# A first stage on one core: the order of its first and last tiles, and its results stored by SyncE's queue instead of GpSimd's

## The reference, cut to what matters

```python
def _L0_cond_ref(x, adapter_mapping, W, b, lora_As, lora_Bs):
    base_out = jnp.einsum('bti,oi->bto', x, W) + b
    A = lora_As[adapter_mapping]          # one of 32 adapters for each batch row
    Bm = lora_Bs[adapter_mapping]
    lora_h = jnp.einsum('bti,bir->btr', x, A)
    lora_out = jnp.einsum('btr,bro->bto', lora_h, Bm)
    return base_out + lora_out * SCALING

x = x + _L0_ffn_ref(_L0_cond_ref(x, itok_B_0_23, ...), L0_ffn_W_gate, L0_ffn_W_up, L0_ffn_W_down)
x = x + _L1_ffn_ref(_L1_cond_ref(x, itok_B_0_7, ...), ...)
```

## Time and profile before

| | |
|---|---|
| median of 3 runs | 974.24 us (974.02 to 5092.53) |
| the profiled execution | 974.92 us |
| its span, first to last instruction | 973.2 us |
| TensorE busy | 964.7 us, 99% of the span |
| VectorE, ScalarE, GpSimd busy | 62%, 49%, 29% |
| granted clock of TensorE | 1.00 of full speed |
| DMA, mean over the span | 229 GB/s |

### The profile page before, as it was taken

The page is one execution under the profiler, slowest core; times in us unless marked ns, Lnnn a source line. Parts: engine busy times, 40 slices in busy tenths (PEclk is TensorE's granted clock), DMA queues, the critical chain, the costliest instruction groups (busy, mean ns, idle before and its releaser), DMA issues.

```text
span 973.2 us, 14085 instructions
## 1 busy us (share of the span) xinstructions
PE 964.7 (99%) x4659; PEld 814.8 (84%) x4659; DVE 605.5 (62%) x1027; ACT 472.1 (49%) x877; POOL 285.8 (29%) x380
## 2 busy tenths in 40 slices
PE   9999999999999999999999999999999999999998
PEld 7888888888888888888888888888888999898986
DVE  5785987877973333785332497333378487785862
ACT  4765766664832333671333383333357274535342
POOL 5984225544202611500713220351150460000000
PEclk9999999999999999999999999999999999999999
DMA  7787476776879876877877768986688650616132
GB/s 238 269 334 263 129 259 237 294 284 237 312 264 321 281 195 194 280 259 254 292 247 196 241 225 266 323 281 193 192 291 289 244 190 23 238 46 215 65 108 87
DMA packets 112081, 222.78 MB, mean 229 GB/s; under 512 B 12165, under 2 KB 12166, under 8 KB 111370
## 3 DMA queue, kind: packets, MB, share of 16 engines
q1 hardware_dynamic: 108576, 211.37, 65.0%
q0 software_dynamic: 3296, 10.51, 3.0%
q10 hardware_dynamic: 138, 0.01, 0.0%
HBM read 160.49 MB, written 61.34 MB: 228 GB/s over the span
## 4 chain that ended last, share of the span: by engine, by line
PE 91%; DVE 3%; POOL 2%; DMA 2%; issue 1%; SPq 0%; POOLq 0%; ACT 0%; ACTq 0%; DVEq 0%
PE bank L2132 90%; POOL a_raw L1001 2%; DMA a_table<-in_a_cols 1%; DMA c_scratch<-c_out 1%; PE bank L2302 1%; SPq L653 0%; DVE cop_lo L1693 0%; POOL c_scratch L1047 0%; POOLq L992 0%; POOLq L1000 0%; DVE xa L1594 0%; POOL b_raw L907 0%; DVE wring L1660 0%; DVE hg L1911 0%; DVE h_masked L1634 0%
## 5 line engine op out<-in xcount | busy, mean ns | idle before, releaser
L2132 PE MATMUL bank<-cop_hi,wring 128*128 128x512 f32 x1234 | 380.4, 389 | 0.0
L2132 PEld LDWEIGHTS bank<-cop_hi,wring 128*128 128x128 f32 x1234 | 231.6, 188 | 48.1
L2132 PE MATMUL bank<-cop_lo,wring 128*128 128x512 f32 x616 | 239.6, 389 | 0.0
L2132 PE MATMUL bank<-op_hi,wring 128*128 128x512 f32 x560 | 173.7, 389 | 0.0
L1739 DVE TENSOR_TENSOR v<-bank,p7s 128x512 f32<-128x512 f32 x44 | 30.4, 692 | 197.1 <-PE bank L2132 197.1
L2132 PEld LDWEIGHTS bank<-cop_lo,wring 128*128 128x128 f32 x616 | 115.6, 188 | 24.0
L2132 PEld LDWEIGHTS bank<-op_hi,wring 128*128 128x128 f32 x560 | 105.1, 188 | 21.8
L2132 PE MATMUL bank<-op_lo,wring 128*128 128x512 f32 x280 | 108.9, 389 | 0.0
L1243 ACT ACTIVATE s<-bank 128x512 f32<-128x512 f32 x44 | 26.3, 597 | 114.2 <-PE bank L2132 114.2
L2132 PE MATMUL bank<-xa,w_hi 128*128 128x512 f32 x256 | 76.1, 391 | 1.1 <-ACT c_out L1140 1.1
L947 POOL TENSOR_TENSOR h_t<-h,h 128x512 f32<-128x512 f32 x20 | 27.3, 1365 | 162.2 <-DVE h L1761 162.2
(11 more groups left out here) (253 smaller groups left out, 1844.4 us busy)
## 6 DMA issues: line engine op xcount, KB each, us to landing
wring<-wgu_scratch SPq DMA_DIRECT2D x231, 256.0 KB, 3.0
wring<-wd_scratch SPq DMA_DIRECT2D x140, 256.0 KB, 5.7
wgu_scratch<-wring SPq DMA_DIRECT2D x77, 256.0 KB, 3.4
xs_raw<-x_scratch SPq DMA_DIRECT2D x16, 512.0 KB, 5.8
out<-res SPq DMA_DIRECT2D x32, 256.0 KB, 2.1
wd_scratch<-dt SPq DMA_DIRECT2D x14, 512.0 KB, 4.9
x_raw<-in_x SPq DMA_DIRECT2D x13, 512.0 KB, 5.9
c_scratch<-c_out POOLq DMA_DIRECT2D x24, 256.0 KB
```

The source lines that it names most:

```text
L2132: return e.matmul(out_ap, lhs, rhs, start=start, stop=stop, skip_group_check=True)
```

## The change

It has five edits; TensorE's program is not touched.

1. SyncE, start: block k = 2 of x of tile 1 is loaded behind `a_table` instead of ahead of it.
2. The stores of c go from GpSimd's program to SyncE's. In a tile they alternate with `store_down`; `load_down(1)` comes behind the stores of tile 1; the seven `store_gate_up` and `load_gate_up(2)` come behind the stores of the last tile.
3. GpSimd: the three small loads (b0, b1, languages) are issued ahead of the first gather; `load_slots` and `pick_a` of tile t + 3 follow the gather of tile t + 2.
4. ScalarE and VectorE, tiles 0 and 1: `lora_turn(0, (0,))` and `lora_in(0, (0,))` ahead of `turn_b(0)`; `turn_a(1, (1,))` ahead of the first `close_c`; `turn_b(1)` behind the second `close_c` on ScalarE and behind `turn_a(1, (1,))` on VectorE; `lora_turn(1, (1,))` ahead of the third `close_c`.
5. VectorE, last tile: of the four `gate_up_lo` that stood ahead of `lora_in(7)`, two come between `lora_in` and `lora_rest`, the other two and `gate_up_sums(1)` behind the operands of the second stage.

```diff
--- before.py
+++ after.py
@@ -571,8 +571,7 @@
 
     def ab_hi_n(t, what, g):
 
-        order = "a0", "b0", "b1", "a1"
-        return 2 * NG * t + (order if t == 1 else sorted(order)).index(f"{what}{g}") + 1
+        return 2 * NG * t + ("a0", "a1", "b0", "b1").index(f"{what}{g}") + 1
 
     def a_n(t, g=NG - 1):
         return NG * t + g + 1
@@ -824,9 +823,11 @@
             load_x(0, ks)
             part = slice(ks[0], ks[-1] + 1)
             e.dma_start(w0_raw[:, part, :], w0[:, part, :]).then_inc(w0_in[ks[0]], DMA)
-            load_x(1, ks[:1])
+            if ks[0] < 2:
+                load_x(1, ks)
         e.dma_start(a_table[:, :, :], a_cols).then_inc(a_table_in, DMA)
-        load_x(1, [KC - 1])
+        for ks in x_parts(1)[2:]:
+            load_x(1, ks)
         for t in range(NT):
             if t == 0:
                 for ks in x_parts(2):
@@ -841,15 +842,19 @@
                 e.wait_ge(b_in, NG * DMA * 2)
                 for ks in x_parts(3):
                     load_x(3, ks)
-            if t < 2:
-                load_down(t)
-            if t == NT - 1:
-                for n in range(7):
-                    store_gate_up(n)
-                load_gate_up(2)
-            for m in range(KC):
-                for n in d_due(t, m):
+            if t == 0:
+                load_down(0)
+            for r, m in enumerate(close_order(t)):
+                if t not in KEPT:
+                    e.wait_ge(c_closed, c_turn(t, m))
+                    e.dma_start(c_dram[TILE_AT[t], m], c_out[m][:, :]).then_inc(c_stored[m], DMA)
+                for n in d_due(t, r):
                     store_down(n)
+            if t == 1:
+                load_down(1)
+        for n in range(7):
+            store_gate_up(n)
+        load_gate_up(2)
 
         load_down_late()
         for n in range(7, N_G):
@@ -1025,6 +1030,10 @@
         e.iota(expert_i[:, :], [[1, E]], base=0, channel_multiplier=0).then_inc(pool_const, 1)
         e.wait_ge(slot_list_in, DMA)
         load_slots(0)
+        e.dma_start(b0_sb[:, :], b0).then_inc(small_in, DMA)
+        e.dma_start(b1_sb[:, :], b1).then_inc(small_in, DMA)
+        lang_rows = langs.unsqueeze(1).to_broadcast([P // SEQ, SEQ, n_lang_cols])
+        e.dma_start(lang_i[:, :], lang_rows).then_inc(small_in, DMA)
         e.wait_ge(w0_in[2], DMA)
         gather(0)
         e.wait_ge(a_table_in, DMA)
@@ -1032,21 +1041,15 @@
         load_slots(1)
         pick_a(1)
         gather(1)
-        e.dma_start(b0_sb[:, :], b0).then_inc(small_in, DMA)
-        e.dma_start(b1_sb[:, :], b1).then_inc(small_in, DMA)
-        lang_rows = langs.unsqueeze(1).to_broadcast([P // SEQ, SEQ, n_lang_cols])
-        e.dma_start(lang_i[:, :], lang_rows).then_inc(small_in, DMA)
+        load_slots(2)
+        pick_a(2)
 
         for t in range(NT):
             if t + 2 < NT:
-                load_slots(t + 2)
-                pick_a(t + 2)
-            for m in close_order(t):
-                if t not in KEPT:
-                    e.wait_ge(c_closed, c_turn(t, m))
-                    e.dma_start(c_dram[TILE_AT[t], m], c_out[m][:, :]).then_inc(c_stored[m], DMA)
-            if t + 2 < NT:
                 gather(t + 2)
+            if t + 3 < NT:
+                load_slots(t + 3)
+                pick_a(t + 3)
 
         for s in range(NS):
             for j in range(NF):
@@ -1350,23 +1353,23 @@
             split_w0(k)
             split_x(1, (k,))
         turn_a(0)
+        lora_turn(0, (0,))
         turn_b(0)
-        lora_turn(0, (0,))
         lora_hi(0, (0,))
         lora_turn(0, (1,))
         turn_a(1, (0,))
         lora_hi(0, (1,))
-        turn_b(1)
         lora_turn(1, (0,))
+        turn_a(1, (1,))
         e.wait_ge(small_in, 3 * DMA)
         e.wait_ge(w0_lo_done, KC)
         close_c(0, 0)
-        turn_a(1, (1,))
         close_c(0, 1)
+        turn_b(1)
         lora_hi(1, (0,))
+        lora_turn(1, (1,))
         close_c(0, 2)
         close_c(0, 3)
-        lora_turn(1, (1,))
         split_x(2, (0, 1))
         lora_hi(1, (1,))
         split_x(2, (2, 3))
@@ -1944,15 +1947,15 @@
                 linked(e.tensor_scalar(row_i[:, :], slot_i[:, :], float(R), r_f[:, 0:1], ALU.mult, ALU.add))
                 assert links[0] == ROWS
         turn_a(0)
+        lora_in(0, (0,))
         turn_b(0)
-        lora_in(0, (0,))
         lora_rest(0, (0,))
         lora_in(0, (1,))
         turn_a(1, (0,))
         lora_rest(0, (1,))
-        turn_b(1)
         lora_in(1, (0,))
         turn_a(1, (1,))
+        turn_b(1)
         lora_rest(1, (0,))
         lora_in(1, (1,))
         split_x(2, (0,))
@@ -1966,6 +1969,9 @@
                 lora_in(t, range(NG))
                 if t < NT - 1:
                     split_x(t + 1, (0,))
+                else:
+                    for n in gate_due(t)[:2]:
+                        gate_up_lo(n)
                 lora_rest(t, range(NG))
                 if t < NT - 1:
                     split_x(t + 1, (1, 2, 3))
@@ -1994,8 +2000,8 @@
                 turn_b(t + 1)
             if t == NT - 3:
                 gate_up_sums(0)
-            if t == NT - 2:
-                for n in gate_due(t + 1):
+            if t == NT - 1:
+                for n in gate_due(t)[2:]:
                     gate_up_lo(n)
                 gate_up_sums(1)
         for n in range(7, LEAD):
```

## The result

| | before | after |
|---|---|---|
| median of 10 runs each | 974.24 us | 977.08 us (975.94 to 978.44) |
| ratio, 95% interval | | 1.0028 (1.0019 to 1.0036) |
| the profiled execution, its span | 974.92, 973.2 | 976.55, 974.8 |

One of the ten executions of before took 5092.53 us; it does not move the median. The forecast was 972.7 with a range of 971.4 to 975.9. The time left the range on the slow side: the change costs 0.28%, well within the 2% that was forecast, but the sign was forecast wrong.

A forecast was written before the change was run, and what follows sets the result against it. TensorE, busy nearly the whole span, was taken to bound the kernel. Terms -0.3 - 0.8 - 1.06 + 0.7 = -1.5 us took the median from 974.24 to 972.7, range 971.4 to 975.9.

The forecast's parts named there:

- behind the last tile: Start of second stage: gate/up load of j = 2, issued behind c stores, delays begin_y; cost 0.7 us.
- third rival: Second stage: weights of j = 2 come late, +1.7 us, 975.9; decides if wu lands after 146.6; chance 0.19.
- The bound of this term: Second stage, late load of j = 2: cost 2.7 us at most, if wg takes 6.1 from its issue.
- Tile 3: TensorE's wait ahead of tile 3 vanishes because tile 1's c stores go out from about 40 us; gain 0.8.
- the forecast's own signs of being wrong: Whole kernel: tile 2 beginning later than 39.54, close_c still waiting for a landing, or brackets past 150 us.
- The second rival: First stage: start loses 0.6, or c stores behind x land after 52.8 and 0.8 stays; 973.6, chance 0.13.
- The start: Up to tile 2: gains 0.5 and 0.5, costs 0.3 and 0.4, so 0.3 us gained.
- Edit 4's gains and its new wait: Tiles 0 and 1: waits at 24.38 and 33.57 give 0.5 each; late lora_hi(1, (1,)) adds 0.4.
- 20.02 grows: Start: TensorE's wait at 20.02 lengthens as x k = 2 lands behind a_table, near 16.3; cost 0.3.
- The last tile: Last tile: VectorE masks h sooner, so TensorE's wait ahead of cond_lora goes; gain 1.06 us.
- nothing beyond 170 us would move: From 170 to 950 us TensorE lacks 0.2 us in 780, so nothing off TensorE can gain there.
- the whole prize: All TensorE idle times named ahead of 170 us, with what drawn ends hide: 4.2 us, 0.4% of the time.

The follow-up runs named there:

- exp. 4: Kernel before with only VectorE's order in the last tile changed (low parts and sums moved later): 972.87 us, ratio 0.9988.
- exp. 8: Kernel before with only ScalarE's and VectorE's orders changed in tiles 0, 1 and the last tile: 972.41 us, ratio 0.9983.
- exp. 9: Kernel of exp. 8 with c stores on SyncE's queue, the last tile's behind the seven stores and load of j = 2: 972.91 us, ratio 0.9986.
- exp. 7: Kernel of exp. 2 with block k = 2 of x of tile 1 loaded ahead of A's table again: 973.16 us, ratio 0.9989.
- exp. 2: Changed kernel with the seven gate/up stores and load of j = 2 ahead of the last tile's c stores again: 973.88 us, ratio 0.9999.
- after (1): The changed kernel run once more, unedited: 976.79 us, ratio 1.0031 to the kernel before.
- experiment 11: Kernel of exp. 8 with only block k = 2 of x of tile 1 put behind A's table: 973.73 us, ratio 0.9996.
- experiment 3: Kernel before with SyncE made to wait for the last close_c before the seven stores and load of j = 2: 978.51 us, ratio 1.0047.
- experiment 6: Changed kernel with only the load of j = 2 ahead of the last tile's c stores, the seven stores still behind: 978.82 us, ratio 1.0042.
- experiment 5: The kernel before once more, unedited, one execution for a second trace: 974.28 us, span 972.5.
- experiment 10: Kernel of exp. 8 with GpSimd's new order (small loads first, A picked behind the gather), c stores still on GpSimd: 972.84 us, ratio 0.9992.

## Why the prediction was wrong

Six kernels, after the last of them, form a ladder in which each kernel differs from the one above by one part of the change. The step is the difference of the ratios times 974.2.

| kernel | adds | ratio (95%) | step, us | forecast |
|---|---|---|---|---|
| exp. 4 | edit 5 | 0.9988 (0.9979 to 0.9997) | -1.2 | -1.06 |
| exp. 8 | edit 4 | 0.9983 (0.9974 to 0.9992) | -0.5 | -0.6 |
| exp. 9 | edit 2, the block in its old place | 0.9986 (0.9977 to 0.9995) | +0.3 | -0.8 |
| exp. 7 | edit 3 | 0.9989 (0.9980 to 0.9998) | +0.3 | 0 |
| exp. 2 | edit 1 | 0.9999 (0.9990 to 1.0008) | +1.0 | +0.3 |
| after (1) | the block behind the last tile | 1.0031 (1.0019 to 1.0043) | +3.1 | +0.7 |

The steps add to +3.0 and the forecasts to -1.5. The ratios' intervals are about 0.9 us to each side, those of a step wider, so of single steps only the last stands well clear; the first has an interval of its own below 1, and edit 1's is given twice (1.0 here, 1.3 in experiment 11) with a mechanism in the trace.

**The step that failed first: "behind the last tile", +0.7.** The mechanism was right (load late, sums late, `begin_y` late, a bracket in j = 1), and so was the moment: the last `close_c` ends at 135.49, which is the 136.84 of before less 1.35, and the block starts at 135.88. The size of the term was wrong, by the landing. It reckoned 144.4 and 145.1 for wg and wu; in the same time base they came at 146.0 and 146.9. Two of its figures were short. The rate of 385 GB/s was the row of another stretch; the mean up to the landing was 322 here and 339 in experiment 1. And the nine transfers of 2.36 MB were not all that moved until then, it was 2.98 MB here and 3.3 in experiment 1. From there each later link took what was forecast. The third rival had put its turning point at a landing of wu after 146.6 in the old time. It came 0.3 past that, and the first stage had given back 1.35 in the profile, not 2.2, so the sum turned. The bound of this term was 2.7; the measured idle of 2.23 with its 0.15 lies inside. With these two figures the forecast's sum would be -1.35 + 2.4 = +1.05, 975.3 for the median and still inside the range. The rest, 1.8, is the load of j = 3 (0.3 in the trace of after, 1.7 in experiment 3), 0.3 more of the second stage without a cause, the 0.7 by which the profiled execution of before stood above its median, and the 0.5 of the next paragraph.

**Not in the forecast at all: the clock.** A term that is an idle time was charged at its own length. Experiments 1 and 6 charge it 1.7 and 2.9 us more. In the profile of after, with an idle of 2.23, there is no such loss (clock 1.00 in every stretch), in experiment 1, with 2.72, there is. It is not why the range failed: the 7 of the 10 runs of after with a clock of 1.00 have a median of 976.55, which is outside as well. The medians lie 2.8 apart and the profiled executions 1.6, since the one of before was 0.7 above its median and the one of after 0.5 below. That 0.5 may be the clock: the three runs with 0.998 took 977.45 to 978.44 and lift the median from 976.55 to 977.08. In experiment 1 the two kinds of run don't part so (976.46 and 976.83 are runs with 0.998), so ten runs are no proof.

**Tile 3, -0.8: the effect is there, the size was wrong.** The seven profiles with the c stores on GpSimd's queue have waits of 0.65, 0.28, 0.33 and 0.25 ahead of tile 3 (before, experiments 5, 10, 11) and three times none (3, 4, 8), on average 0.3 with the drawn ends; the six with the stores on SyncE's queue (after, 1, 2, 6, 7, 9) have none. So the prize was 0.3 where one profile had said 0.8. After's c stores of tile 1 went out from 42.66 (46.70 in before, 40 by forecast). They were not sooner because the stores of tile 0, which the forecast had not looked at, were late: `close_c` of tile 1 waited for them 2.26 and 0.72 us, which is one of the forecast's own signs of being wrong.

```profile
41.94 0.69 ACT L1143 ACTIVATE c_out<-bank,b 128x512 f32<-128x512 f32 x1 [2.26 <-DMA c_scratch<-c_out]
...
43.35 0.69 ACT L1143 ACTIVATE c_out<-bank,b 128x512 f32<-128x512 f32 x1 [0.72 <-DMA c_scratch<-c_out]
```

The second rival had it that c stores land late behind x on one queue, and for tile 0 the traces lean its way. Of its last store eight profiles show the landing: 6.9 to 7.9 us after the issue on SyncE's queue (after, 1, 2, 9), 5.3 to 6.4 on GpSimd's (3, 4, 8, 10). In tile 1 it is the other way: 5.4 to 6.8 on SyncE's, 7.6 to 8.8 on GpSimd's. ScalarE waits for them 1.5 to 3.0 us in all in the six profiles with edit 2, and 0.6 or not at all in the seven without; TensorE has no bracket from it in any of them. From 34.0 to 55.7 us the DMA engines of after move 307 to 429 GB/s in every slice of 1.55 us, so what was issued earlier has to be worked off first. The forecast took from the Trainium skill (DMA: Bandwidth & Descriptors, section "SWDGE vs HWDGE vs iDMA") that the two kinds of queue take turns inside a DMA engine. It reckoned 2.7 us of later landing from that. The 2 us of tile 0 go that way, the 2 us of tile 1 against it; no run here varies the queue alone with the rest of the traffic held, so the rule is neither shown nor refuted.

**The start, -0.3: wrong in one term.** Edit 4's gains and its new wait came as reckoned in the traces; its step of -0.5 is within the intervals. "20.02 grows", 0.3, was too small: x k = 2 landed near 16.7 (16.9 in after), not 16.3, and the splits on VectorE behind ScalarE's made a wait ahead of the base product as well (0.66), which the forecast had no row for. Edit 1 is 1.0 to 1.3. It doesn't always show: experiments 1 and 2 have no bracket there, experiment 6 has 0.83, after 0.93, experiment 11 1.03 and 0.66. Tile 2 began later than 39.54 in after (39.68), the forecast's sign of being wrong here, and sooner in experiments 1 and 2 (38.72 and 38.93).

**The last tile, -1.06: right.** Measured -1.2, and in the profile of after 1.2 between tile 3 and `cond_lora` (75.73 in place of 76.91).

Right as well were, for the change, the claim that nothing beyond 170 us would move, and that the whole prize was small: the best kernel gained 1.7 of the 4.2 us.

Still open: what edit 3 costs (0.3 or 0.9 by its two pairs, each inside the intervals); why experiment 9 and experiment 7 differ at j = 2, 10.04 and 10.69, though SyncE's order is the same in both; what else the DMA moved before the load of j = 2 landed, and what made the gap in its rate; and from what idle on the clock falls in this kernel, of which there are five idle times here and no series.

## What to carry to other kernels

A block of stores and loads that is moved to a later place on a queue has two deadlines, when its first store must free a buffer and when its load must land; price both with the mean rate of a stretch of the same mix, count what is issued behind the load as well, and if a few tenths decide the sign, widen the range past the turning point with all that follows it. A single wait of TensorE of near 3 us can cost 0.6 to 0.9 of itself again in clock (1.7 after 2.72, 2.9 after 3.36), so four small waits are not worth one long one. Brackets in a stage that starts up come and go between runs of one kernel: look at a second profile before a term rests on one.

## What the runs showed of the hardware

- The granted clock fell to 0.50 after TensorE had been idle for 2.72 us (1.7 us lost) and in an idle time of 3.36 us (2.9 us lost while it worked), and stayed at 1.00 after idle times of 2.23 and of 1.93 and 1.69. In experiment 1 it fell only when TensorE had worked for 0.6 us again (between 149.25 and 149.50). It rose while TensorE was at work, near 152.8 there and near 148.8 in experiment 6. The Trainium skill, TensorE: Matmul & The Clock Gate, section "Part 1: The HAM clock gate", says that the half clock is the resting state and activity lifts it. The two traces agree.
- A busy share of the DMA engines near 1.0 is no measure of their rate. In before they moved 403 GB/s at a share of 1.06 (142 to 144 us), in after 374 at 1.01 (138 to 140) and 308 at 1.03 (142 to 144), in half a microsecond of it 254 at 1.07.
- Over 138 to 146 us after has 308 GB/s, experiment 1 335, experiment 2 362 and experiment 8 381, each with another part of the same transfers in that stretch.
- A c store of 256 KB landed 8.0 us (median of twelve) after its issue in the first 62 us of after, and 2.0 to 5.2, median 2.1, from 100 to 135 us.
